# One decoder layer, batch after batch on one core: a scan's skip term moved to TensorE, two projections and one addition moved

## The reference

```python
x = x + mamba(norm(x))                 # the scan
x = x + attention(norm(x), context)    # causal self attention + cross attention, 16 heads of 16
x = x + moe(norm(x))                   # 8 experts, the best 2 per token

# in mamba: 512 channels d, 16 states n, 512 steps t
h[d, n] = exp(delta[d] * A[d, n]) * h[d, n] + delta[d] * B[n] * xs[d]
y[d]    = sum over n of h[d, n] * C[n]
y       = y + xs * D                   # the skip term
y       = y * silu(z)
out     = y @ out_proj

# in attention
y = softmax(causal(q k)) v + softmax(qc kc) vc
out = y @ Wp + bp
```

## Time and profile before

| | |
|---|---|
| median of 3 runs | 1807.3 us (1805.04 to 1811.45) |
| the profiled execution | 1806.43 us, span 1804.6 us |
| granted TensorE clock, mean | 0.925 of 2.4 GHz |
| PE busy | 1459.6 us (81%) |
| DVE busy | 1285.0 us (71%) |
| ACT busy | 818.7 us (45%) |
| POOL busy | 645.6 us (36%) |

### The profile page before, as it was taken

One profiled execution on the slowest core, in us unless ns is written; L12 is line 12 of the kernel. 1 busy time (PEld: TensorE's weight loads), 2 busy tenths in 40 slices (PEclk: granted clock), 3 DMA queues, 4 the chain that ended last, 5 costly groups with the idle time before them and its releaser, 6 DMA issues. The chain is left out here.

```text
span 1804.6 us, 19456 instructions
## 1 busy us (share of the span) xinstructions
PE 1459.6 (81%) x6520; PEld 720.5 (40%) x6520; DVE 1285.0 (71%) x2029; ACT 818.7 (45%) x1586; POOL 645.6 (36%) x630
## 2 busy tenths in 40 slices
PE   5697879995987799877887899945677998589995
PEld 2353522242544232243543222422242223378784
DVE  5998488748996778389985886599948881543324
ACT  3643336756443256664433467453323665222221
POOL 2565341303864322207653322056634021212130
PEclk9899979997999889998998899979997998689998
DMA  4950362003002532021004420030034302157744
GB/s 120 343 159 1 105 138 57 14 13 130 19 1 56 143 67 49 14 94 55 1 10 127 107 58 26 2 132 10 0 95 104 67 26 84 49 160 248 237 153 140
DMA packets 128068, 153.87 MB, mean 85 GB/s; under 512 B 19109, under 2 KB 107694, under 8 KB 125920
## 3 DMA queue, kind: packets, MB, share of 16 engines
q1 hardware_dynamic: 124224, 143.96, 27.5%
q0 software_dynamic: 3744, 8.66, 1.3%
HBM read 102.82 MB, written 50.99 MB: 85 GB/s over the span
## 5 line engine op out<-in xcount | busy, mean ns | idle before, releaser
L170 PE MATMUL PS<-arena 128*32 128x512 f32 (+10 forms) x4150 | 832.0, 450 | 85.0 <-DVE maxs L1849 21.5
L170 PEld LDWEIGHTS PS<-arena 128*32 128x32 f32 (+3 forms) x4150 | 363.9, 128 | 525.4 <-ACT arena L1821 205.6
L1821 ACT ACTIVATE arena<-PS 128x512 f32<-128x512 f32 (+3 forms) x768 | 361.6, 547 | 226.5 <-PE PS L170 225.5
L1404 POOL TENSOR_TENSOR arena<-arena 128x1024 f32<-128x1024 f32 x124 | 292.7, 2362 | 215.6 <-DVE arena L1429 117.1
L1849 DVE TENSOR_REDUCE maxs<-PS 128x1 f32<-128x1024 f32 x256 | 298.0, 1215 | 42.1 <-PE PS L170 41.9
L1429 DVE TENSOR_TENSOR_SCAN arena<-PS,arena 128x1024 f32<-128x1024 f32 x128 | 292.1, 2282 | 0.1
L170 PE MATMUL PS<-arena,ident 128*128 128x512 f32 (+1 forms) x560 | 256.5, 584 | 5.4 <-DVE arena L1438 5.4
L1376 ACT ACTIVATE PS<-arena,A_neg 128x511 f32<-128x511 f32 x256 | 165.9, 681 | 202.8 <-DVE arena L1429 202.6
L1438 DVE TENSOR_TENSOR arena<-arena,PS 128x1024 f32<-128x1024 f32 x128 | 156.3, 1221 | 6.8 <-PE PS L170 2.7
L1565 POOL TENSOR_SCALAR_AFFINE_SELECT arena<-arena 128x128 f32<-128x128 f32 x256 | 73.0, 296 | 235.9 <-ACT arena L1821 232.3
L170 PE MATMUL PS<-bc,bc_sel 96*128 96x512 bf16 x128 | 51.8, 405 | 118.8 <-DVE arena L1438 112.4
(11 more groups left out here) (264 smaller groups left out, 1549.7 us busy)
## 6 DMA issues: line engine op xcount, KB each, us to landing
arena<-in_ew SPq DMA_DIRECT2D x46, 512.0 KB
arena<-stack_parts SPq DMA_DIRECT2D x288, 64.0 KB, 2.3
rows_in<-nil SPq DMA_DIRECT2D x16, 1088.0 KB, 12.6
arena<-b_rows SPq DMA_DIRECT2D x16, 1024.0 KB, 7.7
stack_parts<-arena SPq DMA_DIRECT2D x40, 384.0 KB, 2.6
arena<-stack_parts SPq DMA_DIRECT2D x96, 128.0 KB, 4.3
arena<-rows_in SPq DMA_DIRECT2D x23, 272.0 KB, 5.3
xn<-dens SPq DMA_DIRECT2D x24, 256.0 KB
```

The lines of the kernel that those rows point to most:

```text
L170: return nc.tensor.matmul(o, l, r, start=start, stop=stop)
L1404: nc.gpsimd.tensor_tensor(b_sb[i % 2], u[:, 2 * kh:2 * kh + 2, :], Brow[:, n, :].unsqueeze(1).to_broadcast([P, 2, T]), ALU.mult).then_inc( ...
L1821: nc.scalar.activation(probs[(HG * s + h) % NPR][:, 0:N], ring_bank(n)[:, 0:N], ACT.Exp, scale=HD ** -0.5).then_inc(S["ring_read"], 1)
```

## The change

- **Skip term.** ScalarE builds four 128x128 diagonal matrices D_wide once, before the first scan. In every scan TensorE starts the sums in banks 4 and 5 with D_wide times xs (`skip(kh)`): for kh = 0 ahead of the first unit, behind a wait for `b_ready`; for kh = 1 in the 17th unit, behind the existing wait for VectorE to have read the banks. `gate_channels` is left with one product per tile, from PSUM.
- **Tiles.** `FIRST_TILES` is 8 instead of 6: tiles 6 and 7 are projected, split and stored ahead of the maximum jobs; tiles 8 and 9 follow jobs 1 and 3 instead of 5 and 7. On SP `load_max_rows(0, CAUSAL)` now stands ahead of stores 8 and 9, where it stood ahead of store 9.
- **bp.** GpSimd adds bp to x1 after the first group's division instead of after the first group's masks.

```diff
+        D_wide = sb("D_wide", [P, DT, P])
...
                     if b == 0:
                         act.wait_ge(load_w, 16 * len(FIRST))
+                        act.wait_ge(id_ready, 2)
+                        for m in range(DT):
+                            nc.scalar.activation(D_wide[:, m, :], ident[:], ACT.Copy, scale=D_skip[:, m:m + 1])
                     nc.scalar.activation(table_at[:], dt_b[:, 0:1], ACT.Exp)
...
+                def skip(kh):
+                    for k in range(2):
+                        mm(bank(4 + k), D_wide[:, 2 * kh + k, :], xs[:, 2 * kh + k, :], True, False)
+
                 row(0, 6, "cn_mm")
+                pe.wait_ge(S["b_ready"], 1)
+                skip(0)
                 for i, (kh, n) in enumerate(UNITS):
                     pe.wait_ge(S["g_done"], i + 1)
                     if i + 1 < len(UNITS):
                         row(UNITS[i + 1][1], 6, "cn_mm")
                     if n == 0 and kh >= 1:
                         pe.wait_ge(S["y_read"], 2 * kh)
+                        skip(kh)
                     for k in range(2):
-                        last = mm(bank(4 + k), ident[:], g_sb[i % 2][:, k, :], n == 0, n == NS - 1)
+                        last = mm(bank(4 + k), ident[:], g_sb[i % 2][:, k, :], False, n == NS - 1)
...
                     for k in range(2 * kh, 2 * kh + 2):
-                        nc.vector.scalar_tensor_tensor(delta[:, k, :], xs[:, k, :], D_skip[:, k:k + 1],
-                                                       bank(4 + k % 2), ALU.mult, ALU.add).then_inc(S["y_read"], 1)
-                        dve.wait_ge(S["y_read"], k + 1)
-                        nc.vector.tensor_tensor(u[:, k, :], delta[:, k, :], zs[:, k, :], ALU.mult)
+                        nc.vector.tensor_tensor(u[:, k, :], bank(4 + k % 2), zs[:, k, :], ALU.mult)\
+                            .then_inc(S["y_read"], 1)
...
-            CK_TILES, FIRST_TILES = 2, 6
+            CK_TILES, FIRST_TILES = 2, 8
...
-                for i in range(FIRST_TILES - 1, len(TILES)):
-                    if i == len(TILES) - 1:
-                        load_max_rows(0, CAUSAL)
+                for i in range(5, FIRST_TILES):
+                    store(i)
+                load_max_rows(0, CAUSAL)
+                for i in range(FIRST_TILES, len(TILES)):
                     store(i)
...
-                if b == 0:
-                    pool.wait_ge(S["bp_ready"], 1)
-                link(nc.gpsimd.tensor_tensor(x1[:], x1[:], bp[:].unsqueeze(1).to_broadcast([P, TT, DM]), ALU.add))
                 pool.wait_ge(S["masked"], HG * TT)
                 ones_rows(1)
...
                     nc.gpsimd.tensor_tensor(YT[g], y[0], y[1], ALU.add).then_inc(S["y_ready"], 1)
+                    if g == 0:
+                        if b == 0:
+                            pool.wait_ge(S["bp_ready"], 1)
+                        link(nc.gpsimd.tensor_tensor(x1[:], x1[:], bp[:].unsqueeze(1).to_broadcast([P, TT, DM]), ALU.add))
...
-                project(FIRST_TILES - 1)
+                for i in range(5, FIRST_TILES):
+                    project(i)
...
                     max_job(0, i)
-                    if i % 2:
+                    if i in (1, 3):
                         project(FIRST_TILES + i // 2)
...
                     maxima(0, (i,))
-                    if i % 2 and i < KJOBS - 1:
+                    if i in (1, 3):
                         rest(FIRST_TILES + i // 2)
                 negated_parts(0, CAUSAL)
-                rest(len(TILES) - 1)
                 maxima(0, range(KJOBS, JOBS))
```

More of the change, by code:

```diff
@@ L1796, in scalar @@
                     value_tile(j)
-                for i in range(FIRST_TILES - 1, len(TILES)):
+                for i in range(5, len(TILES)):
                     high(i)
```

## The result

The changed kernel took 1779.5 us (median of 4 runs, 1774.7 to 1783.1) against 1806.2 for the kernel before (the three runs of its table and a fourth): ratio 0.9845, 95% interval 0.983 to 0.986. Run again, unedited, in six later runs it took 1775.3 us (1772.3 to 1783.4), ratio 0.9839 [0.9813, 0.9865]. The forecast was 1780.

The account below looks back on a forecast made before the run. VectorE was taken to bound the scan, with waits between engines in the attention's first part. Savings of 10.4 + 4.7 + 16.4 less 4.5 make 27.0 us, from 1806.4 to 1779.4, as a median 1780 us; range 1769 to 1794.

Parts of the forecast that it names:

- Steps 1 and 2: VectorE's gates in the middle and at the end of each scan get shorter: 10.4 us and 4.7 us saved.
- Step 3: TensorE's added skip products in the scan, and ScalarE's D_wide, stay hidden: cost 0, bound 3 us per batch.
- Step 4: Attention's first stage: tiles 6 and 7 ahead of the maximum jobs save 4.1 us a batch, 16.4 in all.
- The further 0.5 a batch for rest 9: Part of the tiles' 4.1 us: rest 9 no longer stands between the parts and the first context job.
- this idle time, at best, closing: Upper bound for the tiles, 4.9 us a batch, with VectorE's 0.7 us idle in the context jobs mostly closed.
- Step 5: With bp's addition gone from its old place, VectorE's cast meets the second memset: 1.1 us lost a batch, 4.5 in all.
- Step 6: bp's addition after the first group's division: masks slip, a cast may wait; cost 0, at most 0.9 us each.
- a fall only inside the scan: Rival: TensorE's clock falls in the scan, making the kernel slower; 1827 us with 60 units affected, chance 0.03.
- The tiles give little: Rival: the round for rests 6 and 7 slips or group 1 loads come late; 1792 us, chance 0.17.
- The cast isn't held longer: Rival: the cast's place against the memsets moves or no lock holds; 1770 us, chance 0.13.
- The gain was passed on: Denies the rival that later stages are tied to a transfer and the gain isn't passed on; 1797 to 1805, chance 0.06.

Follow-up runs that it names:

- experiment 5: Kernel before with the gate's multiply-add kept on VectorE but writing its result back to PSUM: 1801.2 us, ratio 0.996.
- experiment 1: Kernel before with one part only: skip term 1787.7 us, tiles 1800.3, bp move 1823.8; and the changed kernel with bp back in its old place, 1770.7.
- experiment 4: Changed kernel with group 1's ones-row memsets held until the cast: 1769.7 us; with bp back too, 1768.2; the latter plus five spare TensorE products, 1775.2.
- experiment 6: Changed kernel without TensorE's skip products, D xs not added anywhere: 1774.0 us, ratio 0.9822.
- experiments 1 to 3: experiment 1, then two additions to the kernel with bp moved alone: memsets held until the cast, 1798.3 us; five spare TensorE products in a pause, 1822.4.

## Why the prediction was right, and where it was not

**Total:** 27.0 forecast; 26.7 by the first medians, 31.3 by the second, 29.0 between the spans. The mechanisms of steps 1, 2, 4 and 5 are what the runs show. That the total is as near as 0.3 us is in part luck: single rows of the table err by up to 3.3 us, in both directions, and the errors cancel.

**Steps 1 and 2, the gates:** 15.1 forecast, 15.2 measured, and the reason is shown (experiment 5): the products with a PSUM operand are not stretched, at 0.69 us beside a running GpSimd. The end gates are bounded by TensorE's context pair.

**Step 3, the skip products:** costed at nothing, and nothing it is, in the scan. D_wide's four activations took 1.27 us; ScalarE's dtin then started at 39.97, 0.30 earlier than before.

**Step 4, the tiles:** 3.6 a batch for the first stage, 3.6 measured in the last batch, on whose rows it was built, and 4.2 to 4.3 in the others. The clock goes with this difference: between the first job and parts 1 the granted clock rose from 0.79 to 1.00 in those three, and from 0.80 to 0.89 in the last. The further 0.5 a batch for rest 9 did not come: parts 1 to 2 did not shorten (+0.9 in all). The window over this stretch in the first batch, the kernel before and then the changed one:

```profile
227.64:249.07 21.43, 16.47 (x81) 5.07 (x81) 20.18 (x22) 6.75 (x17) 7.85 (x18) 0.84 0.71 156
```

```profile
217.75:239.71 21.96, 17.97 (x81) 5.36 (x81) 19.71 (x21) 6.14 (x16) 6.62 (x18) 0.77 0.67 161
```

VectorE has one instruction and 0.5 us less to do, but it idles for 2.25 us instead of 1.25. The same 81 products of TensorE take 1.5 us longer, at 0.77 of the clock for 0.84. In the other batches the idle time is 1.8 to 2.1 us for 1.1 to 1.3. The prediction had this idle time, at best, closing. So 16.4 was forecast and 15.5 came.

**Step 5, the cast:** 1.1 a batch forecast, 1.12 in three, 0.70 in the last; the cast 2.63 us as written. Against the changed kernel with bp back the loss is larger, 1.55 in three batches, and the tiles' 0.44 hides it in the table (experiment 1). The rule cited there (the Trainium skill, SBUF — State Buffer, "SBUF: two separate sides"), a lock held for a whole instruction, agrees in both positions, since the cast ends with whichever memset it met, and with the addition that it met in experiment 4. The Trainium skill limits the claim in the same section to a GpSimd that reads when VectorE has two SBUF inputs: the trace agrees too, with 0.28 us for the subtraction at 1358.02 beside a memset, its time where GpSimd stands still as well.

**Step 6, bp's new place:** no cost was seen in parts 4 to 8 (-0.2), though the cast near it took 0.5 to 1.4 us instead of 0.21 in four of eight batches, since the addition held it.

**What no step had:** the level of TensorE's clock outside the scan. I weighed a fall only inside the scan, and in that rival only as a loss. It shows in three places:

- The output projection behind the scan. Shorter gates leave TensorE a shorter pause, 1.45 us for 2.64; in the last batch the 32 products took 7.14 us where they took 8.56. First the changed kernel, then the kernel before:

```profile
1293.36 7.14 PE L171 MATMUL PS<-out_w,arena 128*128 128x256 f32 x32 [1.45 <-PEq L178]
```

```profile
1319.30 8.56 PE L170 MATMUL PS<-out_w,arena 128*128 128x256 f32 x32 [2.64 <-PEq L177]
```

  This and the same in the first batch are most of the -3.3 of the table, and the skip term alone gives them too (experiment 1). Over all 14 profiles these products took 7.14 or 7.15 us in all 32 batches with the short end gate, that of experiment 6 without skip products among them; with the old end gate they did so in 12 of 24 and took 8.56 to 8.83 in the other 12, behind the same pause. So the level stayed up wherever the gate was short; why the longer pause lowers it in some batches only is open.
- Behind the long cast. Windows of 10 us in the first batch, the changed kernel and then that with bp back:

```profile
242.00:252.00 10.00, 7.23 (x30) 3.42 (x30) 7.51 (x17) 2.66 (x5) 6.17 (x3) 0.51 0.29 80
252.00:262.00 10.00, 9.32 (x40) 2.25 (x39) 7.17 (x11) 5.11 (x10) 0.00 (x0) 0.80 0.68 120
```

```profile
242.00:252.00 10.00, 7.67 (x37) 3.55 (x41) 7.37 (x19) 4.03 (x8) 8.60 (x3) 0.66 0.35 95
252.00:262.00 10.00, 9.45 (x52) 2.59 (x45) 9.12 (x11) 5.24 (x11) 0.00 (x0) 1.00 0.60 105
```

  TensorE is busy for 0.4 us less in the first window with the long cast, and the clock is longer at the lower level; parts 3 to 4 took 23.8 us against 22.4. In the kernel before they took 23.8 too, with a cast of 1.5, so this is no price of the cast that could have been added up, and what decides it is as open as in the entry.
- The entry: 4.3 to 6.0 us a batch where the level is low from 62 us behind parts 8 on, mostly 5.7 (experiments 1 to 3). In both profiles of the changed kernel it is none; with bp moved alone the mean clock was 0.911 or 0.912 in all six runs, and the kernel 16.9 us slower than before, where step 5 alone says 4.5. Had the change been this one edit, the forecast built in the same way would have been wrong by 12 us.

**The rivals.** "The tiles give little" is excluded by the rows. "The cast isn't held longer" is excluded for the change as made by the cast's 2.63 us; how near its 1770 such a kernel comes, the ones with the memsets late show, with the cast at 0.21 and 1769.7 and 1768.2 us. A fall of the clock in the scan is excluded by the four scans, at a granted clock of 0.97 to 0.98. The gain was passed on.

**Open:** what decides the level in a batch's entry; and the 2.3 to 2.7 us more from the last parts to the end, which both profiles of the changed kernel show. Over the other kernels this stretch was 310 to 316 us with no order that I can name.

## What to carry to other kernels

An instruction on the path that another engine's instruction blocks ends when that one ends: moving work away from in front of the blocker can move the victim into a longer one. Read which instruction the victim will meet at its new time, and try to put the blocker behind it instead, as the one wait of experiment 4 does (6 to 10 us better than the changed kernel).

Single-edit kernels don't add up when the clock of an engine is not the same in all of them: here -8.9 us for -27. Compare stretch by stretch and set the granted clock beside each before an edit gets the credit or the blame.

A product's second operand in PSUM instead of SBUF cost nothing (0.69 us in both forms) and was worth 0.9 us at three of the four places where GpSimd ran, and 1.5 at the fourth.

## What the runs showed that I had not expected

- A loss of 4.3 to 6.0 us in 13 of 42 entries and of 0 to 1.2 in the others, in a stage in which the change touches no instruction, with the granted clock at 0.50 instead of 1.00 for about 10 us.
- The executions of one program differ by about as much: 1805.8 to 1807.5 us or 1810.5 to 1812.0 in eleven runs of the kernel before, and 1798.1 to 1811.0, with values between, in eleven others.
- Five spare products of 0.13 us in TensorE's pause did not keep its clock up: two of three entries still lost, in each of the two kernels tried.
- The forecast gave 0.5 us a batch for one instruction less on VectorE, and the stretch got longer, with TensorE's clock lower there.
